# A Perceiver block on one core: the expert gate taken from unnormalized rows, two program blocks joined, updates moved from VectorE to ScalarE, and the last stage reordered

## The chip, the cores and the metric

The kernel runs on one core of one Trainium2 chip. A core has five engines with a queue of instructions each: TensorE (PE; PEld is its loading of weights), VectorE (DVE), ScalarE (ACT), GpSimd (POOL) and SyncE (SP), which here issues most of the DMA transfers. They run side by side and wait for each other through semaphores; within one queue the order is fixed. The metric is device time in microseconds (us), the median of several runs; lower is better.

## The reference, cut to what matters

The input x is 64 x 32 rows of 256 numbers, 2048 rows in all. Three residual steps follow each other:

```
x = x + cross_attention(layernorm(x), ctx_768)             # 16 heads, 257 keys each
x = x + attn(layernorm(x))                                 # causal over the 64 positions
x = x + ffn(layernorm(x))                                  # 8 experts, the best 2 of each row

attn: hp = tanh(inputs @ W); scores = hp @ proj            # softmax over earlier positions
      out = tanh(concat(inputs, context) @ concat_w.T + concat_b); out[:2] = inputs[:2]
ffn:  gate = softmax(x @ Wg.T); top 2, divided by their sum
      h = x @ W1[e].T + b1[e]; a, b = split(h)
      eo = (a * sigmoid(b)) @ Wo.T + bo; out = sum over the 2 chosen of eo * weight
```

Here `layernorm` is (x - mean) / sqrt(variance + 1e-05) of each row. The gate is a product of normalized rows with 8 columns, so it equals (x @ Wg.T - mean * columnsum(Wg)) / sqrt(variance + 1e-05). The divisor is positive and one number for each row, so it doesn't change which two experts are the largest.

## The kernel before, in words

The rows are held in SBUF as `xb`, 16 tiles of 128 rows. The program has three stages that matter here, after the cross-attention.

**Self-attention and gate**, four chunks `c` of four tiles each (512 rows), in a hand-written software pipeline of six steps `k`. In step `k` chunk k has its rows normalized (`normed`, on ACT), turned by TensorE (`turned`) and split in two parts (`highs` on ACT, `lowered` on DVE). Chunk k-1 goes through `hidden` (matrix product), `squashed` (two tanh of 128x512 on ACT), `logits`, `masked`, `exps`, `weighted`, `products`, `direct`, `crossed`, `weights`, `mixed` and `outs` (the two closing tanh on ACT). Chunk k-2 has its third residual step: `third` adds the tanh into `xb` and takes the row statistics (DVE), `scales` makes their reciprocal roots (POOL), `final_norm` writes normalized rows `yn` (two or three tiles on DVE, the others on ACT), `store_y` sends them to DRAM (`y_d`), `lifted` turns them, `gate_in` copies them from PSUM (ACT), `gated` multiplies with the gate's weights, `gate_out` copies the result (ACT), `turned_back` turns it again, and `best` and `chosen` find the two experts (DVE). `kept` adds the normalized first two positions into `xb` (one DVE instruction a chunk). Each engine runs its own list of these calls, in program order: on TensorE `hidden`, `turned`, `logits`, `products`, `direct`, `lifted`, `crossed`, `gated`, `mixed`, `turned_back`.

**Routing**: `rank` counts on TensorE how many earlier rows chose each expert, `positions` and `marks` make one-hot marks of 16-bit numbers on DVE (`Bv` and `A16`, in two halves a chunk), `slots` multiplies them so that every place of the sorted list gets its row number, and one more product with `sel` gives `inv`, the rows' list. Chunks 0 to 2 are done in the first program block; chunk 3, the thresholds (`th`, `tb16`, `tb0`, `sel`) and `inv` come after a boundary between two program blocks, at which all engines meet.

**Experts and combination**: 39 groups `i` of 128 rows of one expert. POOL gathers the rows `Xg` from `y_d` by `inv` (it waits for the fourth y store), TensorE turns them (L1810) and multiplies with the expert's weights W1 (12 products, L1825), ACT and DVE make the gated unit, SP stores the result to `g_d`. Then for each of 16 tiles `j` POOL gathers the two expert results of each row (`cg`, L1636, two gathers, at most three tiles ahead of `back`), DVE scales the first (L1750) and adds the second (L1753), TensorE turns the sum (`back`, L1836) and multiplies with Wo (L1853), DVE adds the residual (`final`, L1665), SP stores it. Both gathers of a tile count up one semaphore, and `fo` has four buffers.

SP's order in the first block matters: the weights of experts 0 to 4, bias rows 5 to 7, expert 5, the y stores of chunks 0 to 2, then

```
                sp.wait_ge(u_o, 8)
                load_expert(6)
                load_expert(7)
                store_y(3)
                sp.wait_ge(u_b2, 4)
                for e in range(5):
                    load_bias(e)
```

Each `load_expert` moves 2 MB; `u_o` reaches 8 when the last `mixed` is done. All of these transfers go through one DMA queue.

Of the kernel before, what the change touches and what calls it, by code (L numbers as in the profile page):

```python
# [22 lines left out]
E, HF = 8, 512  # L23
# [52 lines left out]
def build(nc, d, out, vx_d, w1_d, y_d, g_d):  # L76
    ctx = ExitStack()
    with ctx:
# [786 lines left out]
        oht = put("oht", [128, 2, 4, E], F16)  # L865
# [3 lines left out]
        rf = put("rf", [128, 2, 2, 4])  # L869
# [8 lines left out]
        gc = put("gc", [128, 128])  # L878
# [3 lines left out]
        bb = put("bb", [128, E, 1024])  # L882

# [34 lines left out]
        u_iv = sem("u_iv")  # L918
        f_st = sem("f_st")
# [7 lines left out]
        f_g = sem("f_g")  # L927
        f_gm = sem("f_gm")
        f_gc = sem("f_gc")
# [3 lines left out]
        f_yv = sem("f_yv")  # L933
        f_hv = sem("f_hv")
# [9 lines left out]
        for k in range(6):  # L944
# [15 lines left out]
            if k == 5:  # L960
                uses += [(("idle",), u_o, 8), (("r", 2), u_rk, 3)]
# [4 lines left out]
            if 0 <= k - 2 < 4:  # L966
                uses += [(("g", k - 2), f_gl, k - 1)]
        place = {u[0]: n for n, u in enumerate(uses)}
# [4 lines left out]
        def by_vector(c):  # L973

            return 3 if c == 3 else 2

        def on_scalar(c):

            return 4 * c + 2

        pI = B[7]

# [16 lines left out]
        def slots(t, c):  # L999

            for k in range(2):
                t.wait_ge(u_ab, 2 * c + k + 1)
                for j in range(4 * k, 4 * k + 4):
                    mm = t.matmul(pI[:, 0:128], Bv[:, j, :], A16[:, j, :], start=(c == 0 and j == 0),
                                  stop=(c == 3 and j == 7), skip_group_check=True)
            mm.then_inc(u_iv, 1)

        def positions(v, link, c, b):
# [11 lines left out]
            link(v.tensor_copy(rf[:, :, :, :], rq[:, :, :, :]))  # L1020
            link(v.tensor_tensor(T16[:, :, :], i16[:, 0:16].unsqueeze(1).broadcast_to([128, 8, 16]),
                                 rf[:, 1, :, :].rearrange("p k j -> p (k j)").unsqueeze(2).broadcast_to([128, 8, 16]),
                                 ALU.is_equal))

        def marks(v, c):
# [3 lines left out]
            for k in range(2):  # L1029
                v.tensor_tensor(Bv[:, 4 * k:4 * k + 4, :].rearrange("p j (e t) -> p j e t", t=16),  # L1030
                                oht[:, k, :, :].unsqueeze(3).broadcast_to([128, 4, E, 16]),
                                T16[:, 4 * k:4 * k + 4, :].unsqueeze(2).broadcast_to([128, 4, E, 16]), ALU.mult)
                v.tensor_tensor(A16[:, 4 * k:4 * k + 4, :], i16[:, :].unsqueeze(1).broadcast_to([128, 4, 128]),  # L1033
                                rf[:, 0, k, :].unsqueeze(2).broadcast_to([128, 4, 128]), ALU.is_equal).then_inc(u_ab, 1)

        with nc.Block() as block:

            @block.sync
            def _(sp):
# [30 lines left out]
                sp.wait_ge(u_b2, 4)  # L1070
# [4 lines left out]
            def _(t):  # L1075
# [98 lines left out]
                def lifted(c):  # L1174
                    for h in range(2):
                        b = take("t3", c, h)
                        for j in range(4):
                            if j < by_vector(c):
                                t.wait_ge(f_yv, 2 * c + j + 1)
                            else:  # L1180
                                t.wait_ge(f_yn, 2 * c + j + 1 - by_vector(c))
                            mm = t.transpose(b[:, 128 * j:128 * j + 128], yn[:, j, 128 * h:128 * h + 128], ident)
                        mm.then_inc(f_t, 1)

                def gated(c):
                    b = take("g", c)
                    for h in range(2):
                        if c < 3:
                            t.wait_ge(f_hi, 2 * c + h + 1)
                        elif h == 0:  # L1190
                            t.wait_ge(f_hi, 7)
                        else:
                            t.wait_ge(f_hv, 1)
                        for j in range(4):
# [709 lines left out]
```

## Time and profile before

| | us |
|---|---|
| median of three runs | 626.54 (625.04 to 626.72) |
| the profiled execution | 622.39 |
| its span, first to last instruction | 620.6 |

| stretch of the span (us) | stage |
|---|---|
| 0 to 343 | cross-attention |
| 343 to 418 | self-attention and gate, until the last `mixed` |
| 418 to 439 | gate and routing of the last chunk, until the first gather of rows |
| 439 to 561 | experts, 39 groups |
| 561 to 620 | combination |

In the rows below a time at the start of a line is microseconds from the span's first instruction. A line names an engine, its line in the kernel, the operation, what it writes and reads, and how many instructions are merged into it (xN); the bracket at its end is the engine's idle time before it and what ended it. An entry named SPq is SP's queue issuing a transfer, not the transfer itself. PEclk is the granted share of TensorE's full clock of 2.4 GHz.

### The profile page before, as it was taken

The numbers are of one execution on the slowest core, as the hardware profiler recorded it, in microseconds if no ns is written. First come the engines' busy times: TensorE is split into PE (matmuls) and PEld (weight loads), VectorE is DVE, ScalarE is ACT, GpSimd is POOL, SyncE is SP. The second block draws the span as 40 slices with busy tenths as digits, with TensorE's granted clock in tenths as the row PEclk, the third lists the DMA queues.
The fourth block names the chain that finished last, engine by engine and source line by source line (L and its number), as shares of the span: only waits on it lengthen the run. The fifth ranks groups of instructions, "written<-read, shape, count | busy, mean of one in ns | idle before, by whom it ended". The sixth has DMA issues, their size and how long they took to land. (4 is left out here: it accounts for less than half of the span.)

```text
span 620.6 us, 21697 instructions
## 1 busy us (share of the span) xinstructions
PE 595.0 (96%) x8364; PEld 482.7 (78%) x8364; DVE 461.0 (74%) x1081; ACT 335.3 (54%) x735; POOL 321.9 (52%) x474
## 2 busy tenths in 40 slices
PE   8999999999999999999999999996899999998886
PEld 3788878888788887888887688883578888884665
DVE  4687877888678886777777675999789987773553
ACT  3677868878687786788766156541122333330221
POOL 3357858787578777678874311111333333314761
PEclk9999999999999999999999999996999999999999
DMA  8624543776355845774400795119534433434774
GB/s 230 171 64 115 165 162 108 245 175 207 113 189 156 217 149 170 198 232 152 146 4 3 314 407 232 35 35 360 196 128 140 137 128 127 132 124 131 226 238 118
DMA packets 65205, 102.10 MB, mean 165 GB/s; under 512 B 15409, under 2 KB 42097, under 8 KB 64081
## 3 DMA queue, kind: packets, MB, share of 16 engines
q1 hardware_dynamic: 59808, 86.42, 43.3%
q0 software_dynamic: 4432, 13.50, 7.9%
q8 instruction: 69, 1.13, 0.8%
q10 hardware_dynamic: 864, 0.79, 0.5%
q14 instruction: 32, 0.25, 0.2%
HBM read 69.42 MB, written 31.26 MB: 162 GB/s over the span
## 5 line engine op out<-in xcount | busy, mean ns | idle before, releaser
L537 DVE TENSOR_SCALAR Pm<-scores 128x514 f32<-128x514 f32 x128 | 88.1, 688 | 57.2 <-PE scores L750 57.1
L653 ACT ACTIVATE Pm<-Pm,nm 128x257 f32<-128x257 f32 x256 | 115.8, 506 | 2.5 <-DVE nm L542 2.5
L542 DVE TENSOR_REDUCE nm<-Pm 128x2 f32<-128x514 f32 x128 | 87.5, 684 | 2.2
L1623 POOL DMA_INDIRECT Xg<-y_d,inv x39 | 37.2, 954 | 87.5 <-PE scores L1810 70.8
L648 ACT ACTIVATE PT<-bank 128x512 f32<-128x512 f32 x64 | 38.3, 598 | 75.2 <-PE bank L761 75.2
L731 PE MATMUL bank<-hA,wH 128*128 128x258 f32 x256 | 75.3, 305 | 0.1
L738 PE MATMUL bank<-wH,hA 128*128 128x256 f32 x256 | 74.2, 301 | 0.5 <-DVE PT L549 0.5
L761 PE MATMUL bank<-cst,Pm 128*128 128x128 f32 x512 | 70.0, 279 | 0.0
L731 PE MATMUL bank<-hA,wL 128*128 128x258 f32 x256 | 69.2, 281 | 0.0
L738 PE MATMUL bank<-wL,hA 128*128 128x256 f32 x256 | 68.9, 280 | 0.0
L1825 PE MATMUL bank<-W,xh 128*128 x208 | 66.7, 401 | 1.3 <-DVE xl L1733 1.3
L1777 ACT ACTIVATE sg<-sg 128x512 f32<-128x512 f32 x39 | 24.7, 632 | 77.6 <-DVE sg L1650 77.6
L440 POOL TENSOR_TENSOR Mb<-Os,rc 128x64 f32<-128x64 f32 x64 | 21.7, 339 | 78.6 <-DVE rc L562 78.2
L777 PEld LDWEIGHTS bank<-Vs,PT 128*32 128x32 f32 x4096 | 41.3, 110 | 25.8 <-issue 25.0
L761 PEld LDWEIGHTS bank<-cst,Pm 128*128 128x128 f32 x512 | 54.8, 140 | 2.8 <-issue 0.8
L631 ACT ACTIVATE kT<-bank,bcol 128x258 f32<-128x258 f32 x128 | 53.5, 470 | 2.8 <-PE bank L731 2.6
L738 PEld LDWEIGHTS bank<-wH,hA 128*128 128x128 f32 x256 | 48.1, 188 | 2.4 <-DVE PT L549 0.7
L731 PEld LDWEIGHTS bank<-hA,wH 128*128 128x128 f32 x256 | 48.4, 189 | 1.0 <-issue 1.0
L731 PEld LDWEIGHTS bank<-hA,wL 128*128 128x128 f32 x256 | 48.5, 189 | 0.2 <-issue 0.2
L777 PE MATMUL bank<-Vs,PT 128*32 128x17 f32 x4096 | 47.7, 186 | 0.7 <-issue 0.7
L738 PEld LDWEIGHTS bank<-wL,hA 128*128 128x128 f32 x256 | 48.2, 188 | 0.0
L1636 POOL DMA_INDIRECT cg<-g_d,pi x32 | 31.8, 992 | 28.9 <-DMA g_d<-gg 17.0
(261 smaller groups left out, 1425.7 us busy)
## 6 DMA issues: line engine op xcount, KB each, us to landing
w_d<-whl SPq DMA_DIRECT2D x64, 256.0 KB, 3.4
W<-w_d SPq DMA_DIRECT2D x8, 2048.0 KB, 15.6
g_d<-gg SPq DMA_DIRECT2D x39, 256.0 KB, 2.4
wst<-in_W1T SPq DMA_DIRECT2D x32, 256.0 KB, 3.7
cx<-in_ctxT SPq DMA_DIRECT2D x31, 258.0 KB, 2.9
cx<-in_ctxT SPq DMA_DIRECT2D x62, 129.0 KB, 3.4
bb<-in_b SPq DMA_DIRECT2D x8, 512.0 KB, 12.8
xb<-in_x SPq DMA_DIRECT2D x4, 512.0 KB, 4.9
```

What stands on the lines that cost most here:

```text
L537: v.tensor_scalar(Pm[:, i % 2, 2 * p:2 * p + 2, :], S4[:, 2 * p:2 * p + 2, 0:NK], -CLAMP, CLAMP, ALU.max, ALU.min).then_inc(s_cl, 1)
L542: v.tensor_reduce(nm[:, i % 2, 2 * p:2 * p + 2], Pm[:, i % 2, 2 * p:2 * p + 2, :], AX.X, ALU.max, negate=True).then_inc(s_nm, 1)
L631: a.activation(kT[:, i % 2, m, :], held("k", i, m)[:, 0:NKP], ACT.Identity, bias=bcol[:, 2 + m:3 + m]).then_inc(s_ke, 1)
L648: a.activation(PT[:, i % 2, 0, :, :].rearrange("p a b -> p (a b)"), held("p", i, 0)[:, :], ACT.Copy).then_inc(s_pte[0], 1)
L653: a.activation(Pm[:, i % 2, g, :], Pm[:, i % 2, g, :], ACT.Exp, bias=nm[:, i % 2, g:g + 1]).then_inc(s_ex, 1)
L731: mm = t.matmul(b[:, 0:NKP], w[:, 128 * m:128 * m + 128], c, start=(e == 0), stop=(e == 4))
L738: mm = t.matmul(b[:, C * c:C * c + C], x[:, 128 * c:128 * c + 128], w[:, C:2 * C], start=(e == 0), stop=(e == 4))
L761: mm = t.transpose(b[:, o:o + 128], Pm[:, i % 2, 2 * p + gg, 128 * c:128 * c + 128], ident)
L777: mm = t.matmul(pO[r, VH * g:VH * g + VH], PT[:, i % 2, p, 2 * gg + c, r], Vs[:, i % 4, c, 4 * (h // 2) + g, h % 2, :], start=first, stop= ...
L1623: g.indirect_dma_start(out=Xg[:, i % 3, :], out_offset=None, in_=y_d, in_offset=bass.IndirectOffsetOnAxis(ap=inv[:, i:i + 1], axis=0)).the ...
L1636: g.indirect_dma_start(out=cg[:, j % 4, k, :], out_offset=None, in_=g_d, in_offset=bass.IndirectOffsetOnAxis(ap=pi[:, k, j:j + 1], axis=0) ...
L1825: mm = t.matmul(o, x[:, i % 2, k, :], W1[:, bass.DynSlice(w + (part * 2048 + k * 1024 + 512 * h), 512)], start=(k == 0 and part == 0 and x ...
```

## The change

**Gate from the rows as they are.** `lifted` turns `xb` itself, in two pairs of tiles, as soon as the third residual step has written them. `gated` takes the turned rows as weights (128x128) and streams the 8 columns of Wg; in the first chunk it also makes the column sums. `best` subtracts mean times column sum. `gate_out` and `turned_back` go, and the scaling by the reciprocal root is applied to the differences of the logits, in the routing's tail. **Norms and `kept` on ScalarE.** All four tiles of `final_norm` and four instructions of `kept` a chunk run on ACT, at the end of each step behind `outs`; POOL makes the two factors of `kept` (`keep`). **One block.** Routing of chunk 3, the thresholds and `inv` move ahead, the two blocks become one, `best`(3) and `chosen`(3) come right behind those of chunk 2; TensorE gets filler products (`busy`) in other places. **Marks.** Half of the `A16` marks of chunks 2 and 3 are made on ACT (`columns`: four Abs and one Relu). **SP.** The load of WoT waits for the gate and the y stores; `sp.wait_ge(u_b2, 4)` goes. **Combination.** Each of a tile's two gathers has a semaphore of its own, `fo` has 16 buffers, and the last products are put in another order.

```diff
 def marks(v, c):                                  # DVE
+                mine = c < 2 or (c == 3) != (k == 1)
...
+                if mine:
+                    ins = v.tensor_tensor(A16[:, 4 * k:4 * k + 4, :], ...
+        def columns(a, c, k):                     # ACT
+            for j in range(4 * k, 4 * k + 4):
+                a.activation(A16[:, j, :], i16[:, :], ACT.Abs, scale=-1.0, bias=rf[...]).then_inc(u_aa, 1)
+            a.wait_ge(u_aa, 4 * (c - 1))
+            a.activation(A16[:, 4 * k:4 * k + 4, :], ..., ACT.Relu, scale=-1.0, ...).then_inc(u_as, 1)
                 def store_y(c):                   # SP
-                    sp.wait_ge(f_yn, min(2 * c + 2, 7))
-                    sp.wait_ge(f_yv, 2 * c + by_vector(c))
+                    sp.wait_ge(f_yn, 4 * c + 4)
...
-                sp.wait_ge(u_b2, 4)
                 def lifted(c):                    # PE
+                    for p in range(2):
+                        t.wait_ge(u_x3, 2 * c + p + 1)
+                        for h in range(2):
+                            for jj in range(2):
+                                mm = t.transpose(b[:, o:o + 128], xb[:, 4 * c + 2 * p + jj, 128 * h:128 * h + 128], ident)
                 def gated(c):                     # PE
-                            mm = t.matmul(b[32 * j:32 * j + 32, 0:128], WgT[:, h, :], gh[:, h, 128 * j:128 * j + 128],
+                    if c == 0:
+                        for h in range(2):
+                            t.matmul(b[:, 64:64 + E], cst[:, C_ONE:C_ONE + 128], WgT[:, h, 0:E], ...
+                    for p in range(2):
+                        t.wait_ge(f_hi, 2 * c + p + 1)
+                        for jj in range(2):
+                            for h in range(2):
+                                mm = t.matmul(b[:, o:o + E], gh[:, p, x:x + 128], WgT[:, h, 0:E], ...
-                    if 0 <= k - 2 < 4:
-                        turned_back(k - 2)
+                busy(1)
+                rank(t, 2, take("r", 2))
+                rank(t, 3, take("r", 3))
+                busy(4)
                 slots(t, 2)
+                slots(t, 3)
+                busy(1)
+                t.wait_ge(r_sel, 2)
+                t.matmul(b[:, 0:40], iT[:, :], sel[:, :], start=True, stop=True).then_inc(r_i, 1)
+                busy(2)
                 def best(c):                      # DVE
-                    v.wait_ge(f_g, c + 1)
-                    v.tensor_copy(gl[:, k, :], ...
+                    v.wait_ge(f_mv, 4 * c + 4)
+                    v.tensor_tensor(um[:, :, :], bc(mv[:, k, 0]), s8[:, :]..., ALU.mult).then_inc(f_um, 1)
+                    v.wait_ge(f_gm, c + 1)
+                    v.tensor_tensor(gl[:, k, :], bank("g", c)[:, 0:4 * E]..., um[:, :, :], ALU.subtract).then_inc(f_gl, 1)
...
-                    if k < 4:
-                        kept(k)
                     if k == 5:
                         best(2)
                         chosen(2)
-                    if 0 <= k - 2 < 4:
-                        final_norm(k - 2)
+                        best(3)
+                        chosen(3)
...
+                positions(v, link, 3, bank("r", 3))
+                marks(v, 3)
+                ...                               # th, tb16, tb0, sel, iT, inv as in the second block before
                 def final_norm(c):                # ACT
-                    for j in range(by_vector(c), 4):
+                    for j in range(4):
+                def kept(c):                      # ACT
+                    a.wait_ge(u_k, 2 * c + 2)
+                    a.wait_ge(u_xn, 4 * c + 2)
+                    for n in range(4 * c, 4 * c + 4):
+                        a.activation(xb[:, n, :], xb[:, n, :], ACT.Identity, bias=kb[:, n:n + 1], scale=ka[:, n:n + 1]
+                                     ).then_inc(u_b2, 1)
                 # ACT, step k
-                    if 0 <= k - 2 < 4:
-                        final_norm(k - 2)         # stood behind exps
...
                     if 0 <= k - 1 < 4:
                         outs(k - 1)
+                    if 0 <= k - 2 < 4:
+                        final_norm(k - 2)
+                    if k < 4:
+                        kept(k)
+                columns(a, 2, 0)
+                columns(a, 3, 1)
                 # combination, DVE
-                    v.wait_ge(c_g[j % 4], 32 * (j // 4 + 1))
+                    v.wait_ge(c_g[0][j % 4], 16 * (j // 4 + 1))
                     v.tensor_scalar(zc[:, j % 2, :], cg[:, j % 4, 0, :], cmb[:, 0, j:j + 1], ...
+                    v.wait_ge(c_g[1][j % 4], 16 * (j // 4 + 1))
                     v.scalar_tensor_tensor(out=zc[:, j % 2, :], in0=cg[:, j % 4, 1, :], ...
                 # combination, PE
+                for j in range(NTILE - 3):
+                    back(j + 1)
+                    product(j, range(4))
+                product(NTILE - 3, range(4))
+                back(NTILE - 2)
+                product(NTILE - 2, range(2))
+                back(NTILE - 1)
+                product(NTILE - 2, range(2, 4))
+                product(NTILE - 1, range(4))
```

## Rows read from the trace of the kernel before

**Rows 1.** The page, part 1: busy us, share of the span, instructions.

```profile
PE 595.0 (96%) x8364; PEld 482.7 (78%) x8364; DVE 461.0 (74%) x1081; ACT 335.3 (54%) x735; POOL 321.9 (52%) x474
```

**Rows 2.** The chain that ended last: start us, us, what.

```profile
438.35 0.21 DVE inv L1695
...
438.85 3.90 DMA Xg<-y_d,inv
...
607.42 4.17 DMA cg<-g_d,pi
```

**Rows 3.** Timeline of ACT and PE in the self-attention's steps.

```profile
364.01 2.06 ACT L1459 ACTIVATE xn<-xb,nb,rs 128x256 f32<-128x256 f32 x4
...
388.53 0.60 ACT L1512 ACTIVATE zs<-scores 128x512 f32<-128x512 f32 x1 [0.27 <-PE scores L1170]
...
392.17 1.08 PE L1125 MATMUL scores<-hp,bcol 128*64 128x256 f32 x8
...
403.56 0.60 ACT L1512 ACTIVATE zs<-scores 128x512 f32<-128x512 f32 x1 [0.27 <-PE scores L1170]
...
406.77 1.08 PE L1125 MATMUL scores<-hp,bcol 128*64 128x256 f32 x8
```

**Rows 4.** Timeline of PE and PEld: the gate, and two large weight loads.

```profile
385.64 0.80 PE L1195 MATMUL bank<-gh,WgT 128*32 128x128 f32 x16
...
386.50 1.13 PE L1170 MATMUL bank<-Yv,AT 128*128 128x256 f32 x4
...
388.33 0.27 PE L1202 MATMUL bank<-cst,gc 128*128 128x128 f32 x1
...
437.82 0.30 PEld L1798 LDWEIGHTS scores<-sel,iT 128*128 128x128 f32 x2 [1.10 <-DVE iT L1691]
```

**Rows 5.** Timeline of ACT and DVE behind the last mixed.

```profile
418.17 0.60 ACT L1512 ACTIVATE zs<-bank 128x512 f32<-128x512 f32 x1 [0.27 <-PE bank L1170]
...
420.86 0.36 DVE L1355 BATCH_NORM_AGGREGATE mv<-st 128x2 f32<-128x6 f32 x4
...
423.44 0.17 DVE L1383 TENSOR_TENSOR csum<-csum,ms 128x8 f16<-128x8 f16 x1
...
432.29 0.22 DVE L1012 TENSOR_TENSOR pr<-oh,scores 128x64 f32<-128x64 f32 x1
...
436.37 0.28 DVE L1684 TENSOR_TENSOR th<-scores,cst 128x128 f32<-128x128 f32 x1
```

**Rows 6.** Timeline of SP's queue, and the landing of the four y stores (L1049).

```profile
418.17 0.81 SPq L1043 DMA_DIRECT2D W<-w_d  x2
...
424.69 0.37 SPq L1049 DMA_DIRECT2D y_d<-yn  x1
...
DMA to landing us min/median/max: 2.9/2.9/10.0
```

**Rows 7.** Windows: stretch, us, busy (x) of PE, PEld, DVE, ACT, POOL; PEclk, DMA share, GB/s.

```profile
422.00:424.00 2.00, 0.70 (x7) 0.23 (x6) 1.83 (x12) 0.60 (x1) 1.01 (x3) 1.00 0.95 410
424.00:426.00 2.00, 1.88 (x8) 1.42 (x8) 1.79 (x9) 0.60 (x1) 0.00 (x0) 0.63 1.04 442
...
428.00:430.00 2.00, 1.44 (x9) 0.96 (x9) 1.97 (x11) 0.05 (x1) 0.00 (x0) 0.50 1.05 270
...
432.00:434.00 2.00, 2.00 (x9) 0.97 (x9) 1.64 (x9) 0.42 (x2) 0.00 (x0) 0.50 1.02 401
434.00:436.00 2.00, 2.00 (x5) 0.75 (x4) 2.00 (x4) 0.00 (x0) 0.00 (x0) 0.81 1.04 424
```

**Rows 8.** Timeline of the combination's POOL, DVE and PE.

```profile
583.34 0.95 POOL L1636 DMA_INDIRECT cg<-g_d,pi  x1 [0.64 <-issue]
...
603.32 1.29 POOL L1636 DMA_INDIRECT cg<-g_d,pi  x1 [1.25 <-PE scores L1836]
...
611.61 0.49 DVE L1750 TENSOR_SCALAR zc<-cg,cmb 128x512 f32<-128x512 f32 x1 [1.24 <-DMA cg<-g_d,pi]
...
613.43 3.62 PE L1853 MATMUL bank<-WoT,zT 128*128 128x256 f32 x16
```

More of the change, by code:

```diff
@@ L882, in build @@
         bb = put("bb", [128, E, 1024])
+        area(155, 158)
+        Xg = put("Xg", [128, 3, C])
+        area(25.875, 26.03125)
+        inv = put("inv", [128, 40], I32)
+        area(26.21875, 26.3125)
+        tj = put("tj", [128, 3, E])
         u_y = sem("u_y")
@@ L960, in build @@
             if k == 5:
-                uses += [(("idle",), u_o, 8), (("r", 2), u_rk, 3)]
+                uses += [(("idle",), u_o, 8)]
             if 0 <= k - 2 < 4:
@@ L967, in build @@
                 uses += [(("g", k - 2), f_gl, k - 1)]
+            if k == 5:
+                uses += [(("r", 2), u_rk, 3), (("r", 3), u_rk, 4), (("inv",), r_iv, 1)]
         place = {u[0]: n for n, u in enumerate(uses)}
@@ new lines, in build @@
+        area(158, 167)
+        xh = put("xh", [128, 2, 2, 128], F32R)
+        xl = put("xl", [128, 2, 2, 128], F32R)
+        WoT = put("WoT", [128, 4, C])
+        area(199, 207.75)
+        sg = put("sg", [128, 2, 512])
+        gg = put("gg", [128, 2, 512])
+        area(21.625, 22.375)
+        te = put("te", [128, 40, E], F16)
+        area(23.375, 23.875)
+        ew = put("ew", [1, 2, 40], I32)
+        area(26.03125, 26.3125)
+        pi = put("pi", [128, 2, NTILE], I32)
+        area(26.3125, 26.8125)
@@ new lines, in build @@
+        lt = put("lt", [128, E, E])
+        tf = put("tf", [128, 40])
+        area(27, 80)
+        cg = put("cg", [128, 4, 2, 512])
+        zc = put("zc", [128, 2, 512])
+        zT = put("zT", [128, 2, 512])
+        fo = put("fo", [128, NTILE, C])
+        r_pi = sem("r_pi")
+        r_b3 = sem("r_b3")
+        e_x = [sem(f"e_x{i}") for i in range(3)]
+        e_t = sem("e_t")
+        e_hi = sem("e_hi")
+        e_lo = sem("e_lo")
+        e_h = sem("e_h")
+        e_ad = sem("e_ad")
+        e_sg = sem("e_sg")
@@ L1036, in build, with tb, ab @@
+        e_g = sem("e_g")
+        e_gd = [sem("e_gd0"), sem("e_gd1")]
+        c_g = [[sem(f"c_g{k}{i}") for i in range(4)] for k in range(2)]
+        c_z = sem("c_z")
+        c_m = sem("c_m")
+        c_t = sem("c_t")
+        c_te = sem("c_te")
+        c_o = sem("c_o")
+        c_f = sem("c_f")
+        c_out = sem("c_out")
+        def tb(i):
+            return B[2 + i % 2]
+        def ab(i):
+            return [(B[4], B[5]), (B[6], B[7]), (B[0], B[1])][i % 3]
         with nc.Block() as block:
@@ L1174, in lifted @@
                 def lifted(c):
[L1175 to L1182, printed above, removed]
+                    for p in range(2):
+                        b = take("t3", c, p)
+                        t.wait_ge(u_x3, 2 * c + p + 1)
+                        for h in range(2):
+                            for jj in range(2):
+                                o = 256 * h + 128 * jj
+                                mm = t.transpose(b[:, o:o + 128], xb[:, 4 * c + 2 * p + jj, 128 * h:128 * h + 128],
+                                                 ident)
                         mm.then_inc(f_t, 1)
@@ L1514, in gate_in @@
                 def gate_in(c):
-                    for h in range(2 - (c == 3)):
+                    for h in range(2):
                         a.wait_ge(f_t, 2 * c + h + 1)
@@ L1844, in _, with product @@
                 t.wait_ge(e_g, NS)
-                back(0)
-                for j in range(NTILE):
-                    if j + 1 < NTILE:
-                        back(j + 1)
+                def product(j, part):
                     t.wait_ge(c_te, j + 1)
```

263 lines of the change are left out of this document (100 added, 163 removed).

## The prediction

> **What bounds the kernel now.** I read the page first, then the chain that ended last, then timelines of the stretch 343 to 443 and of the combination, windows for the clock, and the landing of transfers. On the page TensorE is busy for 96% of the span [rows 1], so what is put on TensorE, or what it has to wait for, counts, and time is to be had only where it is not the bound. Such places are two. From the last `mixed` (its last product releases the tanh at 418.17 [rows 5]; I call this moment M) to the first gather of rows at 438.85 [rows 2] TensorE mostly waits for VectorE: 20.7 us. And in the combination POOL's gathers and their landing pace everything until the products that end it [rows 2, 8]. Between them lie 39 expert groups that the change leaves alone: they move with their start.
>
> The sum is made against the profiled execution (622.39, span 620.6). That one lies 4.15 us below the median of the runs, 626.54; I carry the difference over to the median.
>
> **Part 1, the pipeline up to M: +6.8.** Two things lengthen it.
>
> *ScalarE.* `final_norm` and `kept` now stand behind `outs`, ahead of the next step's tanh of `squashed`, for which `logits` waits. Four instructions of 128x256 with scale and bias take 2.06 [rows 3], and that is what `kept` and `final_norm` cost each. Before, the last tanh of `outs` starts at 388.53 and takes 0.60, and `logits` starts at 392.17; its second half, which needs the second tanh, is half of 1.08 later, at 392.7 [rows 3]. After, ACT would be at 389.13 + 2.06 + 2.06 = 393.25 and through both tanh at 394.45: 1.8 late, 1.6 with the little by which neighbours on ACT overlap. The next step has the same with 403.56 and 406.77: 403.56 + 0.60 + 4.12 + 1.20 = 409.5 against 407.3 [rows 3], 2.2 late, I take 2.0. TensorE's queue is in order, so `attended`, `products` and `direct` behind `logits` wait as well. In the two earlier steps only `kept` is added; 2.06 fits the slack of the second (392.7 - 389.13 - 1.20 = 2.4), and in the first `normed` stands right ahead of it, which I put at 0.7, between 0 and 2.06. Together 4.3. What VectorE loses (`kept`, part of `final_norm`) gains nothing here, as it is not what TensorE waits for.
>
> *The gate on TensorE.* Before, a chunk's 16 short instructions with weights of 128x32 took 0.80, partly waiting for `gate_in`, and `mixed` came 0.86 after their start [rows 4]. Now each chunk loads 16 times 128x128 of 32-bit numbers. The trace of before has no such run of loads with 8 columns behind them. The bounds are 0.05 each (0.80 / 16) and 0.15 (two large loads in 0.30 [rows 4]); I take 0.11, since the two in the last row overlap. 16 x 0.11 = 1.76 puts `mixed` 0.9 later. `turned_back` goes, about 0.2 of TensorE's time [rows 4], for the first two chunks (the third's stands behind M). The first chunk also makes the column sums, 4 loads, of which part fits the wait for `gate_in`. So 1.0 + 0.7 + 0.9 = 2.5 or so with rounding, between 0 and 4.
>
> At no cost: `keep` on POOL (two tiny instructions a chunk; POOL waits there for statistics, and ACT uses the factors much later; their price without that cover would be some 0.5 a chunk), two more small VectorE instructions in `best` (the copy it replaces waited for `turned_back`), the y stores 0 and 1 later (3 us in a queue that is empty there).
>
> **Part 2, from M to the first gather: -0.85.** VectorE's path first. Before, its statistics end 3.05 after M (420.86 + 0.36) and `best` with `chosen` of one chunk takes from 421.22 to 423.61, 2.4; `positions` and four marks take 4.1 (432.29 to 436.37), and from there to `inv` it is 2.2 (436.37 to 438.56) [rows 2, 5]. After: 3.05 + 2.7 (`best` has two small instructions more) + 2.4 (the last chunk needs no sums) + twice 3.5 (three marks of 0.6 instead of four; the ACT half is made meanwhile and is covered by VectorE's other three) + 2.2 = 17.3. With 0.3 to POOL's issue that is 17.6, 3.1 less than before. The boundary of the blocks, `final_norm`, the copy for the gate and the exponents' preparation drop out of it.
>
> But POOL also waits for the fourth y store. SP loads experts 6 and 7 behind the third y store, and that one now waits for `final_norm` of chunk 2, which runs after the closing tanh: M + 0.60 + 2.06, + 0.37 for SP to issue the store [rows 3, 5, 6]. So 4 MB of weights start 3.0 after M and not at M (418.17 [rows 6]). The fourth y store is queued behind them: issued at 424.69 it landed 10.0 later, where the others need 2.9 [rows 6], at 434.69, 16.5 after the weights' issue, with the DMA engines full [rows 7]. After: M + 3.0 + 16.5 + 0.3 = M + 19.8, later than VectorE's path by 2.2, and only 0.85 better than now. This is the wait that takes the place of the one removed. The five bias loads behind it come as much later, and at some 400 GB/s [rows 7] their 2.6 MB take 6.5 us, until about M + 26; their first use is about M + 27 (gather 3.9 [rows 2], turning, splitting and half a group, some 3.5), so nothing, or 1 us if that cover is gone. WoT is used over 100 us later.
>
> **Part 3, the clock at the experts' start: +1.4.** TensorE has `inv` at about M + 17.3 and six filler products behind it, some 2.6 us, and the first gathered rows at M + 19.8 + 3.9 [rows 2]: it idles for over 3 us. In 422 to 424 it was busy for 0.70 of 2 us, and then the granted share went to 0.63 and 0.50, that is 1.2 GHz, and came back within 434 to 436, after it had worked without a pause from about 432.1 [rows 7]: 2.7 us of full work at half speed, a loss of 1.35. I take the same here, with bounds 0 and twice as much.
>
> **Part 4, combination: -2.65.** The first scaling no longer waits for the second gather: 0.49 is off the path at the end (611.61 [rows 8]). At the end 16 instructions of the last two products took 3.62 [rows 8]; a quarter of them, 0.9, now runs ahead of the last `back`, less a wait for the last copy: 0.75. In between, POOL idles 0.30 between gathers, but 0.50 to 1.25 at six tiles of which two stand in [rows 8], where it waits for `back` three tiles before; these six make 2.4 over the usual gap. With 0.5 off that loop five of them go and the largest shrinks; as each step gained moves the next, about 1.6 remain, and 1.4 if faster gathers land a little later (bounds 0 and 2.4). The 16 buffers of `fo` gain nothing, as no wait of VectorE for a store shows at `final`.
>
> **Sum.** +6.8 - 0.85 + 1.4 - 2.65 = +4.7: 627.1 for the profiled execution, 631.2 for the median.
>
> **Rivals.** *A, the transfers keep up.* The stretch 428 to 430 moved only 270 GB/s, others over 400 [rows 7], so the two weight loads may need less than their 15 us once nothing else shares the queue. It decides if the fourth y store lands within 14 us of the weights' issue; then VectorE's path sets the start (-3.1), TensorE hardly idles (part 3 goes), and the sum is 6.8 - 3.1 - 2.65 = +1.1: 627.6, not slower by what can be told. Against it: the DMA share is about 1.0 there as well.
> *B, the clock also falls in the two stalls before `logits`* (1.6 and 2.0 us idle, much like 1.3 of 2 us in 422 to 424 [rows 7]). Twice 1.35 more: 633.9. For it: the only drop within the work followed such idling. Against it: dense work on both sides. [...]
> *C, the combination's pace stays*, because the gathers' landing and not the wait for `back` limits it (4.17 at the end, the longest wait in that part of the chain [rows 2]): 1.4 less gained, 632.6.
> *D, the large weight loads cost no more than the small ones*, 0.05: the gate adds nothing, 2.5 less, 628.7.
> *E, faster than before.* A and D together with all 2.4 of POOL's gaps: 6.8 - 2.5 - 3.1 - 3.65 = -2.45: 624.1.
>
> **How the numbers follow.** The forecast 0.38, A 0.19, B 0.15, C 0.10, D 0.10, E and what I don't see 0.08. A measurement tells differences over 0.3%, 1.9 us: 624.66 and 628.42 are the borders. Slower: forecast 0.36, B 0.15, C 0.10, half of D 0.05, a little of A 0.02, in all 0.68. Within: A 0.16, D 0.04, forecast 0.02: 0.22. Faster: 0.10, E and a part of A and D. The range goes from A with a better combination, 625.8, to B with an unchanged pace, 635.5; the forecast's own is 629 to 633.
>
> **What would show it.** In the changed kernel's trace: idle time of TensorE before `logits` ended by the tanh, 1.5 to 2 us, in the last two steps; the gate's 16 instructions taking 1.7; M at about 425; both weight loads issued 3 us behind M, the fourth y store landing around 444 and the first gather right behind it, while `inv` was ready before; the granted clock below 1 at the first groups; and, in the combination, hardly a POOL gap over 0.3. If `logits` starts on time, or if the first gather follows `inv` at once, the forecast is wrong at that step.

## The result, and the profile after

The changed kernel takes 640.77 us (median of 4 runs, 638.73 to 641.49) against 626.63 for the kernel before: ratio 1.0217, 95% interval 1.0183 to 1.025, so 14.1 us slower. Forecast were 631.2 and a range of 625.8 to 635.5: the direction came, at three times the size, and the time lies above the range. The profiled execution of after took 641.49 (span 639.7).

TensorE's share of busy time hardly moved, as the page's first part shows beside [rows 1]; the loss is in stretches that this share doesn't show.

```profile
PE 605.1 (95%) x8368; PEld 493.9 (77%) x8368; DVE 453.0 (71%) x1072; ACT 350.8 (55%) x767; POOL 323.7 (51%) x482
```

The timeline of ACT and PE in the third step, answering to [rows 3] and [rows 4] (yn is `final_norm`, xb `kept`, hp the tanh that `logits` waits for, L1268 the gate):

```profile
386.24 1.93 PE L1268 MATMUL bank<-WgT,gh 128*128 128x8 f32 x16
...
390.04 0.60 ACT L1588 ACTIVATE zs<-scores 128x512 f32<-128x512 f32 x1 [0.26 <-PE scores L1241]
390.53 2.08 ACT L1541 ACTIVATE yn<-xb,nb,rs 128x256 f32<-128x256 f32 x4
...
392.51 2.07 ACT L1551 ACTIVATE xb<-xb,kb,ka 128x256 f32<-128x256 f32 x4
394.49 1.06 ACT L1559 ACTIVATE hp<-bank 128x512 f32<-128x512 f32 x2
...
395.21 1.08 PE L1196 MATMUL scores<-hp,bcol 128*64 128x256 f32 x8 [1.58 <-ACT hp L1559]
```

Two blocks of four instructions, 2.08 and 2.07, stand between the tanh of `outs` and the next one, and TensorE idles 1.58 for it; in the next step it idles 1.98. The gate takes 1.93 where it took 0.80.

The chain that ended last, from M (now 426.40, the tanh behind the last `mixed`) to the first groups, answering to [rows 2], [rows 5] and [rows 6]:

```profile
426.90 2.08 ACT yn L1541 x4
428.99 3.28 DMA y_d<-yn
432.48 0.38 issue
432.86 1.58 ACT yn L1541 x3
434.46 12.81 DMA y_d<-yn
447.31 0.83 issue
448.14 5.74 DMA Xg<-y_d,inv
...
455.92 5.48 PE bank L1824 x12
```

VectorE isn't in it, for `inv` was ready at 444.24:

```profile
444.04 0.20 DVE L1487 CAST inv<-scores 128x40 int32<-128x40 f32 x1 [0.45 <-PE scores L1318]
```

`final_norm` of chunk 2 runs behind the closing tanh, its store must land before chunk 3 may overwrite `yn`, and chunk 3's store lands 12.81 after its issue. The first group takes 5.48, where before it took

```profile
444.42 3.02 PE bank L1825 x12
```

Windows of after (columns as in [rows 7]) show why:

```profile
410.00:412.00 2.00, 0.67 (x9) 0.45 (x8) 1.73 (x9) 2.00 (x6) 0.19 (x1) 1.00 0.50 172
412.00:414.00 2.00, 1.36 (x10) 0.81 (x11) 0.23 (x1) 0.98 (x3) 1.40 (x4) 0.97 0.27 90
414.00:416.00 2.00, 2.00 (x11) 2.00 (x10) 0.61 (x2) 1.32 (x8) 0.00 (x0) 0.50 0.04 8
...
448.00:452.00 4.00, 0.30 (x1) 0.00 (x0) 1.11 (x6) 0.00 (x0) 3.11 (x3) 0.93 1.04 405
452.00:454.00 2.00, 0.00 (x0) 0.01 (x1) 0.00 (x0) 0.00 (x0) 0.00 (x0) 0.50 0.62 209
454.00:462.00 8.00, 7.43 (x20) 5.35 (x21) 1.99 (x4) 2.84 (x5) 1.89 (x2) 0.52 0.13 40
```

TensorE stood from 448.3 to 454.0, the clock went to 0.50 (1.2 GHz), and the first group ran so. It also fell behind the second stall before `logits`. Last, the combination, answering to [rows 8]:

```profile
593.68 0.66 PE L1835 MATMUL scores<-cst,zc 128*128 128x128 f32 x4 [0.56 <-issue]
...
596.92 0.42 DVE L1687 TENSOR_TENSOR fo<-bank,xb 128x256 f32<-128x256 f32 x1 [3.30 <-PE bank L1849]
596.98 0.60 ACT L1788 ACTIVATE zT<-scores 128x512 f32<-128x512 f32 x1 [3.76 <-remote]
...
597.70 0.95 POOL L1660 DMA_INDIRECT cg<-g_d,pi  x1 [2.00 <-remote]
```

ScalarE's copy follows the start of the four transposes (593.68) by 0.64 to 0.69 at most tiles; here it starts 3.30 after. ScalarE, VectorE and POOL all go on at about 597: they waited for TensorE's signal ("remote" is a releaser that the profile didn't find). I call the time from the start of the transposes to the start of the copy a tile's lag. Three tiles have lags of 2.88 to 3.30, so lose 2.2 to 2.6 us; in [rows 8]'s profile no lag is over 0.70.

The 19.1 us between the two spans, in stretches (us of before, after):

| stretch | before | after | change | predicted |
|---|---|---|---|---|
| start to M | 418.17 | 426.40 | +8.2 | +6.8 |
| M to the first gather | 20.68 | 21.74 | +1.1 | -0.85 |
| gather to the first product of `glu` (gg) | 9.46 | 14.13 | +4.7 | +1.4 |
| to the end of the last gg | 114.19 | 115.02 | +0.8 | 0 |
| combination, to the last fo | 55.01 | 59.41 | +4.4 | -2.65 |

### The profile page after: what moved, and what is told of

Same layout as the page of the kernel before. It is cut to its first block and busy times, and to the rows that moved or that the text cites. A ratio compares the mean times of both kernels' runs of the same rounds, so it can differ in the third digit from the quotient of the medians.

```text
span 639.7 us, 21735 instructions
## 1 busy us (share of the span) xinstructions
PE 605.1 (95%) x8368; PEld 493.9 (77%) x8368; DVE 453.0 (71%) x1072; ACT 350.8 (55%) x767; POOL 323.7 (51%) x482
## 5 line engine op out<-in xcount | busy, mean ns | idle before, releaser
L1824 PE MATMUL bank<-W,xh 128*128 x208 | 68.9, 413 | 0.7 <-DVE xl L1738 0.7
```

The source lines that it names most:

```text
L1824: mm = t.matmul(o, x[:, i % 2, k, :], W1[:, bass.DynSlice(w + (part * 2048 + k * 1024 + 512 * h), 512)], start=(k == 0 and part == 0 and x ...
```

## The experiments

Each is told with its edit, the expectation on record, what came and what follows. Medians are compared with before as measured beside them (626.2 to 627.4); a bracket behind a median holds the ratio to it and its 95% interval.

**1. The combination by itself, twice.** Theory at first: the three alterations cost what the two profiles differ by. The edit takes them out of after, or puts them alone into before:

```diff
-        c_g = [[sem(f"c_g{k}{i}") for i in range(4)] for k in range(2)]
+        c_g = [sem(f"c_g{i}") for i in range(4)]
...
-        fo = put("fo", [128, NTILE, C])
+        fo = put("fo", [128, 4, C])
...
-                for j in range(NTILE - 3):
-                    back(j + 1)
+                for j in range(NTILE):
+                    if j + 1 < NTILE:
+                        back(j + 1)
```

> The changed kernel with the combination as it was before (one semaphore for both gathers of a tile, four buffers of fo, each back ahead of the product before it). Theory 1, the three alterations themselves cost: the changed kernel's combination took 59.4 us from the last gg to the last fo against 55.0 before, so this one takes 55 and the time is 636.5 (640.8 - 4.4). Theory 2, the alterations gain the 2.65 that was predicted, and the three waits of 2.2 to 2.7 us for TensorE's signal that stand in the changed kernel's combination have another cause (that one execution, or where the instructions lie): the same waits, or none, and 640.8 + 2.65 = 643.4.

> The kernel before with the three alterations of the combination alone. Theory 1: 626.6 + 4.4 = 631.0, with waits of over 2 us of ScalarE, VectorE and POOL for TensorE's signal in the combination. Theory 2: 626.6 - 2.65 = 624.0, the combination 52.4 us from the last gg to the last fo, no such waits.

After with the old combination: 638.54 (1.0176, 1.0112 to 1.0241), 59.69 us from the last gg to the last fo, with the waits. Before with the new one: 626.24 (0.9994, 0.9967 to 1.0021), 59.24 us, with the waits. Neither theory: both combinations have the waits and neither is measurably better. The one execution without them was the profile of before.

**2. ScalarE's order.** The hypothesis for the largest part.

```diff
                     if k + 1 < 4:
                         normed(k + 1)
+                    if 0 <= k - 1 < 4:
+                        kept(k - 1)
...
                         weights(k - 1)
+                    if 0 <= k - 2 < 4:
+                        final_norm(k - 2)
                     if 0 <= k - 1 < 4:
                         outs(k - 1)
-                    if 0 <= k - 2 < 4:
-                        final_norm(k - 2)
-                    if k < 4:
-                        kept(k)
```

> The changed kernel with two lines of ScalarE's order moved: kept(k - 1) behind normed, final_norm(k - 2) ahead of outs. Theory: the two instructions of 2.06 us ahead of the next tanh make the stalls before logits and the fall of the clock there, and they put off the third y store, so the weights of experts 6 and 7: the last mixed ends about 5 us earlier (421.4 for 426.4), TensorE waits for no tanh before logits(2) and logits(3) by over 0.5 us, the clock stays full there, the fourth y store lands at about 438 and the first gather starts at 438 to 439 for 448.1; 640.8 - 9 = 631.8 or less. Rival: the gate's 16 loads in each chunk are the larger part (4 x 1.9 us): the last mixed ends at 424 or later and the time is above 636.

629.31 (1.0044, 1.0012 to 1.0077): 11.5 us of the 14.1 gone, by the order alone. (Of the 12.5 between the two spans some 2 lie in the experts and the combination, where nothing was edited.) Its timeline in the third step, and of SP and POOL behind M (420.54):

```profile
392.11 0.60 ACT L1559 ACTIVATE hp<-bank 128x512 f32<-128x512 f32 x1 [0.77 <-PE bank L1176]
...
392.87 1.08 PE L1196 MATMUL scores<-hp,bcol 128*64 128x256 f32 x8
```

```profile
419.55 0.36 SPq L1121 DMA_DIRECT2D y_d<-yn  x1
420.53 0.92 SPq L1116 DMA_DIRECT2D W<-w_d  x2
427.50 0.37 SPq L1121 DMA_DIRECT2D y_d<-yn  x1
...
435.79 0.38 SPq L1629 DMA_DIRECT2D WoT<-in_fWoT  x1
```

```profile
439.64 1.29 POOL L1647 DMA_INDIRECT Xg<-y_d,inv  x1 [14.28 <-DVE inv L1487]
```

Now the tanh waits for TensorE, not TensorE for it. The third y store is ahead of the weights; the fourth has landed when `WoT` goes out (SP waits for it), 8.3 after its issue, and `inv` releases the first gather. From the second tanh of chunk 0's `outs` (373.49) to M it takes 47.05 against 44.32 before (373.85 to 418.17): with the stalls gone, three chunks' gate costs 2.7.

**3. The fourth y store on another queue.**

```diff
-                store_y(3)
...
+                a.wait_ge(f_yn, 16)
+                a.dma_start(y_d.rearrange("(n p) c -> p n c", p=128)[:, 12:16, :], yn[:, :, :]).then_inc(f_yd, 16)
                 a.wait_ge(u_rf, 3)
```

> The changed kernel with the fourth y store issued by ScalarE on its own DMA queue, not by SyncE behind the weights of experts 6 and 7. Theory: the store lands late (12.8 us) because it stands behind 4 MB in one queue; here it lands 3 to 7 us after its issue, at 438 to 442, and the first gather follows inv at about 444.2 for 448.1: 640.8 - 4 = 636.8. Rival: the 16 DMA engines are full, whichever queue it is in: it lands after over 10 us and the time stays within 1 us of 640.8.

640.01 (1.0206, 1.0148 to 1.0265). The rival holds; the chain has it:

```profile
434.46 14.96 DMA y_d<-yn
449.46 0.83 issue
450.29 3.80 DMA Xg<-y_d,inv
```

14.96 against 12.81: another queue gained nothing. The trace shows what the DMA engines did (queue, kind: packets, MB, share of the 16 engines; q1 is SP's queue, q10 ScalarE's with the store alone), from 438 to 442 and from 442 to 448:

```profile
q1 hardware_dynamic: 96, 1.56, 93.6%
q10 hardware_dynamic: 86, 0.09, 6.2%
...
q1 hardware_dynamic: 428, 1.58, 78.9%
q10 hardware_dynamic: 422, 0.42, 20.0%
```

The engines took the packets of the two queues nearly one for one. A packet of the store holds 1 KB, one of the weights 16 KB and one of the biases behind them 4 KB, so the store got 6% and then 20% of the engines. In after the store did stand behind the weights, as the prediction put it: from 434.5 to 442 its queue moved packets of 15 KB on average, none of the store's.

```profile
q1 hardware_dynamic: 195, 2.93, 101.1%
```

So its place in the queue was a reason in after, and to leave that queue was no remedy, for the engines are full either way. The Trainium skill, DMA: Bandwidth & Descriptors, section "Queues, rings and completion order", says that an engine takes turns between the queues that it has work for, a packet at a time; the packet counts agree with it.

**4. Fillers at the experts' start.**

```diff
                 t.wait_ge(r_iv, 1)
-                busy(3)
+                busy(9)
```

> The changed kernel with nine filler products instead of three behind inv, so that TensorE works through the 5.7 us (448.3 to 454.0) in which it waited for the first gathered rows. Theory: the granted clock falls at 451.4 because of that pause; here it stays full through the first groups (2.75 us each and not 5.48), the last gg ends 2.6 to 3 us earlier, 640.8 - 2.8 = 638. Rival: it falls because of the earlier thin work (gate, ranks, slots), or the experts wait for rows and not for the clock: within 1 us of 640.8.

636.2 (1.0157, 1.0092 to 1.0223), 4.6 less. The chain:

```profile
445.91 7.72 PE bank L1796 x18
453.64 0.23 PE scores L1809 x2
...
454.98 3.00 PE bank L1824 x12
```

TensorE works until the rows are there and the first group takes 3.00. From the turning of the rows to the end of the first group: 4.3 (453.64 to 457.98) against 7.4 (454.02 to 461.40); so the clock at the start cost some 3. In the stall before `logits` the clock did not fall in this execution: 408.12 to 425.55 from tanh to tanh, 17.43, against 407.48 to 426.40, 18.92, which is 1.5 less. Nothing was changed there, and little of it arrives: the rows are turned 0.4 sooner. The rest of the 6.0 between the two spans, 0.9 in the experts and 1.7 in the combination, lies where nothing was edited either. With the same code up to `logits` the clock fell there in the profiles of after and of experiment 3, and not in those of experiments 1 (its first kernel), 4 and 5.

**5. The fourth y store ahead of the weights.**

```diff
                 sp.wait_ge(u_o, 8)
+                store_y(3)
                 load_expert(6)
                 load_expert(7)
-                store_y(3)
```

> The changed kernel with the fourth y store ahead of the weights of experts 6 and 7 in SyncE's order. The store in another queue landed no sooner, so its lateness should be the full DMA engines, not the queue. Theory: with no weights under way the store lands 3.3 us after its issue at 434.5, so at 438, and the first gather follows inv at 444.2 (448.1 in the changed kernel); the weights then start at 434.9 and not at 429.4 and are landed only at 450 to 452, the biases at about 457, and the first group waits for them: first gg at 460 to 462 for 462.3, time 639 to 641. Rival: the transfers are not what the start waits for, only the gather is: 4 us earlier, 636.8.

636.82 (1.0175, 1.011 to 1.024). The gather went at 444.57, `inv` releasing it, and:

```profile
446.16 6.27 DMA Xg<-y_d,inv
452.48 0.69 PE scores L1809 x2
...
453.44 5.48 PE bank L1824 x12
```

Of 3.6 us won at the gather 1.1 are lost again: the first group's products start at 453.44 for 455.92, 2.5 sooner. Between M and the first group some 8 MB have to be moved (8.33 from 428 to 452 in after), so what one transfer lands sooner another lands later. The clock fell once more. The median is the rival's 636.8, but not for its reason: of the 4.6 between the spans of the two profiles only 2.5 lie ahead of the first gg, and 1.5 lie in the combination. (Here, too, the clock did not fall before `logits`; that gained nothing, as `inv` came at 444.27, no sooner than in after, behind fillers that ran at half clock.)

**6. What makes TensorE's signals late.** First the output's stores, all issued behind the last fo.

```diff
+                sp.wait_ge(c_f, NTILE)
                 for j in range(NTILE):
-                    sp.wait_ge(c_f, j + 1)
```

> The changed kernel with ScalarE's order of e3_act_order, and the stores of the output all issued behind the last fo. It looks at the three to four waits of 2 to 3 us for TensorE's signal that stand in the combination of every run but the profiled one of before. Theory 1, the output stores cause them: the combination from the last gg to the last fo takes 53 to 54 us for 58.1, and no such wait stands in it. Theory 2, they come from TensorE itself or from the gathers: the waits stay and it takes 57 to 60 us. The time as a whole is longer by what the stores then take at the end, 8 to 12 us.

647.9 (one execution), combination 56.72, two tiles with lags of 3.24 and 3.20: theory 2. The time is 18.6 above experiment 2's and not 8 to 12; why the late stores cost so much stays open. Then the kernel before, for a second profile:

> The kernel before, unchanged, for a second profile. All runs since show three waits of 2 to 3 us for TensorE's signal in the combination, and the profiled execution of before, at 622.39, lies below every other run of that kernel (624.8 and up). Theory: that execution was the exception, and a usual one of before has the waits too, with a combination of 57 to 60 us from the last gg to the last fo for 55.0 there; all else as it was (last mixed releases the tanh at 418, first gather at 438.9). Rival: before has no such waits, they belong to the changed combination: 55 us again.

626.5, span 624.6, M at 417.71, first gather at 438.82, last gg ended at 562.12, and then 59.42 us of combination. Its waits by engine (line, waited for: us, times, longest):

```profile
ACT zT L1782 <- remote: 12.2, 3, 4.2
```

One of these lags, 2.61, in the timeline:

```profile
575.87 0.66 PE L1836 MATMUL scores<-cst,zc 128*128 128x128 f32 x4 [0.46 <-DVE zc L1753]
...
578.48 1.11 ACT L1782 ACTIVATE zT<-scores 128x512 f32<-128x512 f32 x2 [4.17 <-remote]
```

So the profile of before was an exception: 622.39 lies below every other run of that kernel, and its combination lacks 4.4 us of waits that a usual one has. Against this profile the combination of after is 59.41 to 59.42. What makes the waits is asked of two kernels, built on the last one of experiment 8, one execution each:

```diff
-                    for k in range(2):
+                    for k in range(1):
                         g.indirect_dma_start(out=cg[:, j % 4, k, :], ...
```

> The kernel of e13_fewer_fillers that leaves out the second gather of each tile in the combination (both scalings take the first one's rows): half the gathers' traffic, TensorE's work the same and at its own pace. Theory 1, the gathers make TensorE's signals late: no wait of over 2 us for them, the combination takes 43 to 47 us. Theory 2, TensorE itself makes them: the waits stay, as many for as many tiles, and it takes 48 to 54 us.

```diff
                     for m in part:
+                        if m % 2 == 0:
+                            continue
```

> The kernel of e13_fewer_fillers that leaves out half of each tile's product in the combination (two of four parts), the gathers unchanged. Theory 1 (gathers): the waits of 2 to 3 us stay, the combination takes 56 to 59 us. Theory 2 (TensorE's rate): they go, and it takes 51 to 54 us at the gathers' pace.

With half the gathers all 16 copies start 0.64 to 0.69 behind their transposes, no wait is put down to "remote", and the combination takes 46.97. With half the product it takes 57.33, two tiles have lags of 3.01 and 3.04, a third 1.82, and the list of waits has

```profile
ACT zT L1788 <- remote: 8.1, 2, 4.4
```

That speaks for theory 1: the waits go with the gathers, and a slower pace of TensorE's own is not what makes them. It rests on one execution without waits, and of the 17 profiles with both gathers one, the first of before, has none either; so it is likely and not certain. Whether it is the gathers' bytes or their number, and by what path, stays open.

**7. The gate doubled, and one line of two.** The gate's loads and products made twice, on the kernel of experiment 2:

```diff
-                            for h in range(2):
+                            for h in (0, 1, 0, 1):
```

> The kernel of e3_act_order with every load and product of the gate made twice (32 instead of 16 in each chunk, the second overwrites the first with the same values). Theory: a chunk's 16 take 1.93 us and all of it is on the path, so that each chunk's mixed comes 1.93 later: the tanh behind the last mixed at 420.5 + 3 x 1.93 = 426.3 (the fourth chunk's gate stands behind M and moves the first gather by another 1.93), 629.3 + 7.7 = 637. Rival: a part lies in waits (for ScalarE's tanh, for VectorE's scores): under 4 us, below 633.

638.86 (1.0179, 1.0134 to 1.0223), 9.6 more. The four executions lie far apart, 634.05 to 641.88, and the profiled one is the slowest; none is below 633, so the gate is on the path for the most part. In the profile M came at 435.25, 14.7 later and not 5.8. What goes beyond the theory stands beside falls of the clock, in windows:

```profile
384.00:388.00 4.00, 4.00 (x39) 4.00 (x37) 0.00 (x0) 4.00 (x9) 0.00 (x0) 1.00 0.00 0
388.00:390.00 2.00, 2.00 (x11) 2.00 (x11) 0.14 (x1) 0.17 (x1) 0.00 (x0) 0.54 0.45 152
```

It fell with PE busy without a pause, on loads of 128x128 with 8 columns behind each, and so at each of the three chunks ahead of M, for 6.8 us each time. The profile as a whole is 12.9 longer than that of experiment 2 (640.1 for 627.2): from the first gather to the first gg it takes 10.5 for 12.3, and the first group ran at full clock there (3.03 for 4.60).

Then only `kept` moved as in experiment 2:

```diff
+                    if 0 <= k - 1 < 4:
+                        kept(k - 1)
...
                     if 0 <= k - 2 < 4:
                         final_norm(k - 2)
-                    if k < 4:
-                        kept(k)
```

> The changed kernel with kept(k - 1) moved behind normed and final_norm(k - 2) left behind outs. Theory: one of the two blocks of 2.06 us ahead of the next tanh is gone, the stall before logits is below 0.5 us in every step, the clock stays full there and the tanh behind the last mixed comes at 420 to 421; but the third y store still waits for final_norm behind the closing tanh, so the weights start 3 us behind it, the fourth store lands at about 439 to 440 and the first gather starts then: 1 to 2 us above e3_act_order, 630 to 632. Rival, the y stores matter no more once the stalls are gone: 629.3 as e3_act_order.

632.61 (1.0079, 1.0053 to 1.0104): M at 420.64, as in experiment 2, and 3.3 more at the end. So what stood ahead of `logits` makes some 8 us of the loss (8.2 by the medians) and the late y stores 2 to 3 (3.3 by the medians, 2.2 in the profiles up to the first gg: 454.06 for 451.89); the expectation had 1 to 2 for these. The chain:

```profile
423.22 3.34 DMA y_d<-yn
...
428.74 11.11 DMA y_d<-yn
...
440.72 1.21 POOL Xg L1647
```

**8. A better version.** On the kernel of experiment 2, step by step: fillers ahead of `slots(2)` cut from four to one (they had run at half clock for 6.3 us with VectorE and ScalarE waiting behind them), `WoT` loaded in the experts, no filler ahead of `inv`, then fewer behind it.

```diff
-                busy(4)
+                busy(1)
                 slots(t, 2)
...
                 t.wait_ge(r_iv, 1)
-                busy(3)
+                busy(4)
```

> The kernel of e3_act_order with three of its four filler products ahead of slots(2) taken out and one put in behind inv. In e3_act_order these eight instructions ran at half clock and took 6.3 us, and slots(2) waited behind them while VectorE and ScalarE waited 1.9 and 3.6 us for it. Theory: the first gather starts at 437.5 for 439.6, and 629.3 - 2 = 627.3, 1 to 2 less if the clock also stays full at the first groups. Rival: the fourth y store lands last (435.8 in e3_act_order) or the gather's landing takes what is won: 629.

628.01 (1.002, 0.9994 to 1.0046), 1.3 less and not 2: the gather went at 438.79 and not at 437.5, its rows landed 5.67 later.

```diff
                 slots(t, 3)
-                busy(1)
                 b = take("inv")
...
-                busy(4)
+                busy(5)
...
-                sp.dma_start(WoT[:, :, :], d["fWoT"].rearrange("(k p) n -> p k n", p=128)).then_inc(w_o, 16)
                 for i in range(NS):
...
+                    if i == 4:
+                        sp.dma_start(WoT[:, :, :], d["fWoT"].rearrange("(k p) n -> p k n", p=128)).then_inc(w_o, 16)
```

> The kernel of e8_both with two more edits: WoT (0.5 MB, used only in the combination) is loaded behind the fifth group and not among the biases, and the filler product between slots(3) and inv, which took 1.8 us at half clock, stands behind inv. Theory: inv 1.3 us earlier, first gather at 437.5 for 438.8, its rows landed in 4.5 us for 5.7, 628.0 - 2.2 = 625.8, level with before or a little faster. Rival: the fourth y store (436.4 in e8_both) and the biases behind it set the start whatever the queue holds else: within 0.7 of 628.0.

628.02 (1.0028, 1.0012 to 1.0043): the gather went at 437.61, but the fillers behind `inv` ran until 446.0, at half clock until 442.7, and took back what was won: the expectation had not counted them. The next has the edit of experiment 1 as well:

> The kernel of e10_best with the combination as it was before, for a direct comparison of the three alterations. The prediction gave them 2.65 us. Theory, as the waits for TensorE's signal pace the combination in nearly every run, they gain nothing: within 1 us of e10_best. Rival, they gain 2.65 beside the waits: 2 to 3 us slower than e10_best.

629.79 (1.006, 1.0038 to 1.0082), 1.8 above: between the two expectations. In the profiles 1.4 of it lies ahead of M, where the code is the same, and the combinations took 57.67 (new) and 57.51 (old).

```diff
-                busy(5)
+                busy(2)
```

> The kernel of e10_best with two and not five filler products behind inv in the second block. In e10_best they ran at half clock from 437.0 to 446.0 and the gathered rows, landed before that, waited for their end. Theory: first group's last step at 448.3 for 451.2, 628.0 - 2.9 = 625.1, 0.2% below before. Rival: the rows land only at 445 to 446 (5.7 us behind the gather in e8_both), or the first groups run at half clock without the fillers: 627 to 628.

627.13 against 627.38 for before (0.9988, 0.9963 to 1.0014): level, at the rival's lower end. The product for `inv` comes 1.0 sooner behind M than in the first kernel of this experiment (16.3 for 17.3), but the rows take 5.7 as there, with no `WoT` among the transfers:

```profile
436.94 0.64 PE scores L1317 x2
...
438.17 5.72 DMA Xg<-y_d,inv
```

## Why the prediction was wrong, step by step

**Part 1, up to M: mechanism and size right, without the clock.** Where the clock stayed full (experiment 4) it takes 50.73 from chunk 0's tanh to M against 44.32: 6.4 longer. Ahead of it the five profiles of this code up to M are 0.3 to 1.3 later than before (forecast 0.7). Forecast were 6.8 in all. The stalls were 1.58 and 1.98 (forecast 1.6 and 2.0), the gate 2.7 (2.5). The 1.5 more in after's profile is rival B, at one of the two stalls and in two of these five profiles only.

**Part 2, to the first gather: the chain right, the sizes off by 1.9.** `final_norm` behind the tanh, the weights 3.0 behind M, the fourth store landing last, VectorE ready before: all there. But the store landed 17.9 after the weights' issue and not 16.5, and POOL followed after 0.83 and not 0.3. That the store stood behind the weights was right (experiment 3); the size failed, and its place in the queue is not all that holds it: on a queue of its own it landed no sooner.

**Part 3, the experts' start: the step that failed most.** It counted 1.35 for the clock and took the gather's landing over from [rows 2], 3.90. The landing was 5.74, with biases and `WoT` under way at 405 GB/s. It is 3.80 in experiment 3, 6.27 in experiment 5, and 5.72 without `WoT` in experiment 8, so it goes with the bytes of the weights and biases; that they cause it is likely, as no run takes them away. And the pause of 5.7 us cost some 3 and not 1.4. The biases' lateness was priced ("nothing, or 1 us"), but as their own use, not as what their bytes do to the gather. Parts 2 and 3 together: forecast +0.55, measured +5.7.

**Part 4, combination: the term that didn't come.** -2.65 was worked out from gaps of an execution that lacked the waits which a usual one has. Set against the second profile of before it gained 0.0, and the medians speak for the new one by 0.7 and 1.8 and for the old one by 2.2 (of which the clock before `logits` may be a part): no sign that holds. The 4.15 us by which the profiled execution lay below the median was seen and only carried over; it was those waits. Rival C, that the pace stays, is what happened. Its reason, the gathers, has something for it: with half of them the combination takes 46.97, 8 us less than even the execution of before without waits. But the late signals, which no rival had, come on top of it.

With the usual execution as the base the parts measure 8.7 to M (forecast 6.8), 0.6 to the gather (-0.85), 5.0 to the first gg (1.4), 0.8 in the experts (0) and 0.0 in the combination (-2.65): 15.1, the two spans' difference, and the forecast misses 3.6 of it at part 3, the most. The 0.8 is 0.17 at the second group and 0.02 us at nearly every one behind it; experiment 1's first kernel and experiment 4 don't have it, so it isn't the change.

**The rule on the clock.** The Trainium skill, TensorE: Matmul & The Clock Gate, section "HAM oscillation — how this bites in real kernels", tells of waits for transfers, longer than the stalls here, behind which each next burst of matmuls starts cold. The experts' start agrees, with a pause of 5.7 us and a granted clock of 0.50 behind it. For the stalls of 1.6 and 2.0 us it decides nothing: behind the first the clock stayed full in all five profiles of that code, behind the second it fell in two. And experiment 7 shows a fall without any wait, which that section does not have.

## What to carry to other kernels

Work moved to an engine with idle time is priced by what stands behind it in that engine's order: the same instructions at other places in ScalarE's list were worth 11.5 us here. In a stretch that hands one stage to the next, add up all bytes under way and not the one transfer that is waited for: reordering moved the wait from the store to the gather. And where the profiled execution is faster than every timed run, find what it lacks before a saving is read from its gaps.

## What the hardware showed that was not expected

TensorE's clock fell to half while it was busy 4.00 of 4 us and 2.00 of 2 us, on large weight loads with 8 columns each. TensorE's signals arrive 1 to 3 us late at two to five of 16 tiles in 16 of 17 profiles with gathers of two times 128 rows per tile, and at none in the one profile with half of them. A store on a queue of its own landed after 14.96 us beside transfers of another queue, where one with none ahead of it takes 2.9 to 3.3: in 4 us 86 of its packets of 1 KB went beside 96 packets of mostly 16 KB.
